# Splat attention with a following FFN on one Trainium2 core: output products due four key tiles sooner, denominators inverted after a block transposition, and another closing part

## The reference

```python
x = L0_attn_x                                   # (4, 2048, 256), float32
x = x + attn(layernorm(x))                      # 16 heads of 16
x = x + ffn(layernorm(x))

# attn: q, k, v from qkv_w; centers, scales, amplitudes of 16 splats for each head
q_weights = exp(q_dists * inv_var)              # squared distance of q to each center
k_weights = exp(k_dists * inv_var)
logits = einsum('bihs,bjhs,hs->bijh', q_weights, k_weights, amplitudes)
attention = softmax(logits / temp, axis=2)
out = einsum('bijh,bjhd->bihd', attention, v).reshape(Bx, Tx, Dx) @ out_w.T

# ffn: a shifted mix of each row with the row before it
xr = mu_r * x + (1 - mu_r) * x_prev;  xk = mu_k * x + (1 - mu_k) * x_prev
r = sigmoid(xr @ W_r.T);  k_act = square(relu(xk @ W_k.T))
out = r * (k_act @ W_v.T)
```

## Time and profile before

| | |
|---|---|
| median of three runs | 2170.7 us |
| profiled execution, and its span | 2168.94 us, 2167.2 us |
| TensorE matmul busy | 2132.7 us, 98% of the span |
| ScalarE busy | 2015.0 us, 93% |
| VectorE busy | 901.6 us, 42% |
| GpSimd busy | 393.0 us, 18% |
| the 2048 exponentials start | from 63.9 to 2125.5 us |
| granted TensorE clock, mean | 0.998 |

### The profile page before, as it was taken

One profiled execution on the slowest core, in us unless ns is written; L12 is line 12 of the kernel. 1 busy time (PEld: TensorE's weight loads), 2 busy tenths in 40 slices (PEclk: granted clock), 3 DMA queues, 4 the chain that ended last, 5 costly groups with the idle time before them and its releaser, 6 DMA issues.

```text
span 2167.2 us, 52662 instructions
## 1 busy us (share of the span) xinstructions
PE 2132.7 (98%) x22996; PEld 979.0 (45%) x22996; DVE 901.6 (42%) x1868; ACT 2015.0 (93%) x2194; POOL 393.0 (18%) x490
## 2 busy tenths in 40 slices
PE   8999999999999999999999999999999999999998
PEld 5444444444444444444444444444444444444445
DVE  6334544344443443444424344326333333424335
ACT  3899999999999999999999999999999999999994
POOL 0244243342100142022101203320310000000001
PEclk9999999999999999999999999999999999999999
DMA  6645435463321344316031432522261041311111
GB/s 179 164 123 151 113 110 123 131 154 104 92 46 47 92 118 101 97 41 179 24 89 29 128 77 87 123 87 79 59 158 52 22 87 50 53 29 50 33 40 49
DMA packets 176474, 193.34 MB, mean 89 GB/s; under 512 B 88640, under 2 KB 108480, under 8 KB 176224
## 3 DMA queue, kind: packets, MB, share of 16 engines
q1 hardware_dynamic: 166960, 174.96, 30.0%
q0 software_dynamic: 7168, 14.69, 2.9%
q10 hardware_dynamic: 2096, 0.14, 0.1%
HBM read 99.03 MB, written 75.94 MB: 81 GB/s over the span
## 4 chain that ended last, share of the span: by engine, by line
PE 90%; ACT 6%; DVE 2%; issue 1%; DMA 0%; SPq 0%; POOL 0%; DVEq 0%; POOLq 0%
PE ps_pv L886 40%; PE ps_scores L867 27%; PE ps_step L914 17%; ACT probs L1206 6%; PE ps_step L935 2%; PE ps_scores L899 1%; PE ps_scores L904 1%; PE ps_step L893 1%; ACT weight L1270 0%; PE ps_scores L909 0%; PE ps_scores L908 0%; DMA attn<-attn_kept 0%; DVE weight L1486 0%; DMA x_prep<-x 0%; DVE ffn_stats L1389 0%
## 5 line engine op out<-in xcount | busy, mean ns | idle before, releaser
L1206 ACT ACTIVATE probs<-ps_scores 128x1024 f32<-128x1024 f32 x2048 | 1940.9, 1031 | 84.0 <-PE ps_scores L867 58.6
L886 PE MATMUL ps_pv<-probs,vals 128*32 128x512 f32 (+5 forms) x10104 | 1079.9, 520 | 0.1
L867 PE MATMUL ps_scores<-q_aug,k_aug 49*128 49x512 f32 x4096 | 707.0, 442 | 8.0 <-ACT probs L1206 5.8
L867 PEld LDWEIGHTS ps_scores<-q_aug,k_aug 49*128 49x128 f32 x4096 | 331.8, 184 | 616.6 <-ACT probs L1206 562.7
L886 PEld LDWEIGHTS ps_pv<-probs,vals 128*32 128x32 f32 x10104 | 349.8, 139 | 200.3 <-issue 116.8
L1336 POOL DMA_DIRECT2D packed<-qk x224 | 113.0, 510 | 872.8 <-DVE qk L1509 851.0
L1341 POOL TENSOR_TENSOR packed<-qk 32x512 f32<-32x512 f32 x224 | 239.6, 1070 | 16.9
L1715 DVE RECIPROCAL den_all<-den_all 128x128 f32<-128x128 f32 x252 | 224.1, 924 | 0.6
L1346 POOL TENSOR_TENSOR k_act<-k_act 128x512 f32<-128x512 f32 x28 | 30.1, 1076 | 815.7 <-DVE k_act L1512 815.7
L1576 DVE COPY o_raw<-ps_pv 128x512 f32<-128x512 f32 x64 | 44.3, 692 | 246.9 <-PE ps_pv L886 246.3
L1486 DVE TENSOR_SCALAR weight<-ps_step,cen_sq 128x512 f32<-128x512 f32 x57 | 42.8, 751 | 185.2 <-PE ps_step L935 184.3
(11 more groups left out here) (218 smaller groups left out, 1116.1 us busy)
## 6 DMA issues: line engine op xcount, KB each, us to landing
k_aug<-k_parts SPq DMA_DIRECT2D x128, 192.0 KB, 4.7
q_aug<-q_parts SPq DMA_DIRECT2D x128, 192.0 KB
k_parts<-parts SPq DMA_DIRECT2D x32, 512.0 KB, 3.1
q_parts<-parts SPq DMA_DIRECT2D x32, 512.0 KB, 4.0
packed<-qk POOLq DMA_DIRECT2D x224, 64.0 KB, 2.3
x_ffn<-x SPq DMA_DIRECT2D x18, 512.0 KB, 4.8
k_parts<-parts SPq DMA_DIRECT2D x32, 256.0 KB, 3.8
q_parts<-parts SPq DMA_DIRECT2D x32, 256.0 KB, 4.4
```

What stands on the lines that cost most here:

```text
L867: mm = pe.matmul(ps_scores[:, g % RING, e, :], k_aug[rows, s % 2, pair, kt * P:(kt + 1) * P], q_aug[rows, u % 2, pair, :], start=True, sto ...
L886: mm = pe.matmul(ps_pv[32 * c:32 * c + 32, at], vals[:, s % 2, kt, :, c], probs[:, tick % PROB_SLOTS, c, at], start=(kt == 0), stop=(kt == ...
L1206: act.activation(probs[:, tick % PROB_SLOTS, 2 * pair:2 * pair + 2, :], ps_scores[:, g % RING, :, :], ACT.Exp).then_inc(probs_ready, 1)
```

## The change

Three things are changed together.

- `OUT_TICKS` goes from (17, 14) to (13, 10). The planner lays out all side work anew from this, so steps of many tasks stand at other ticks from tick 222 to 752 and from 938 to 1016. What stands between and before is as it was.
- The inverse: `spread` becomes a transposition of 32x32 blocks (one 128x512 instruction), after which each denominator stands once in every 32nd column. One reciprocal of 128x16 inverts them at the next tick, and a second transposition, of a broadcast view, spreads them over `den_all`. The multiply comes two ticks behind `spread` rather than six, and the store three ticks behind it rather than seven.
- The closing part: the last unit isn't copied out of `ps_pv` (no `take`); its transposition and its multiplies read PSUM. The last chunk's attn rows of stages 0 and 1 are loaded once, inside the loop (`LAST_ATTN_AT`), and the unit before the last is read from `o_raw`, not from DRAM. The second-to-last chunk's mixes are made by VectorE, not by ScalarE and GpSimd, its k products come ahead of its r products, and the last output rows are gated, finished and stored in three parts (two tiles, one, one) rather than two.

```diff
-OUT_TICKS = (17, 14)
-INVERT_PARTS = 4
+OUT_TICKS = (13, 10)
+LEFT_TICKS = 3
+INVERT_STEPS = 2
+LAST_ROWS = (slice(0, 2), slice(2, 3), slice(3, 4))
+LAST_ATTN_AT = end(LAST_BUT, "out1") + 1
...
@@ sync
-                for u in LEAVE_AT.get(tick - INVERT_PARTS - 3, ()):
-                    store_attn(u)
+                for u in LEAVE_AT.get(tick - LEFT_TICKS, ()):
+                    if UNIT[u] != (LAST[1], STAGES - 2, LAST[2]):
+                        store_attn(u)
+                if tick == LAST_ATTN_AT:
+                    for odd in range(2):
+                        done = UNIT_OF[LAST[1], odd, LAST[2]]
+                        sp.wait_ge(attn_stored[done % 2], ATTN * (done // 2 + 1))
+                    sp.wait_ge(step_mm, STEP_NO[LAST_BUT, "out1"] + 1)
+                    sp.dma_start(out=attn[:, 0, :], in_=attn_kept[LAST[1], 0:P, LAST[2] * CHUNK:(LAST[2] + 1) * CHUNK]
+                                 ).then_inc(attn_loaded, 16)
-            for odd in range(2):
-                sp.wait_ge(attn_stored[odd], ATTN * ((UNITS - 2 - odd) // 2 + 1))
-            sp.wait_ge(step_mm, STEP_NO[LAST_BUT, "out1"] + 1)
-            sp.dma_start(out=attn[:, 0, :], in_=attn_kept[b, 0:P, at]).then_inc(attn_loaded, 16)
-            for c in range(HEADS):
-                sp.dma_start(out=attn[32 * c:32 * c + S, 1, :], in_=attn_kept[b, P + 32 * c:P + 32 * c + S, at]).then_inc(attn_loaded, 16)
@@ tensor, closing part
-            pe.wait_ge(attn_loaded, 16 * n + 16 * (1 + HEADS))
+            pe.wait_ge(attn_loaded, 16 * (n + 1))
+            pe.wait_ge(scaled, UNITS - 1)
-                pe.matmul(banks[t][:, 0:D], attn[:, 1, t * P:(t + 1) * P], wout_last[:, 0, :], start=False, stop=False)
+                pe.matmul(banks[t][:, 0:D], o_raw[:, (UNITS - 2) % 2, at], wout_last[:, 0, :], start=False, stop=False)
-            pe.wait_ge(pv_free, UNITS)
-            pe.wait_ge(last_added, 2)
-            closing("r0", 7)
-            closing("r1", 6)
+            pe.wait_ge(last_mixed, 3)
+            closing("k0", 7)
+            closing("k1", 6)
             pe.wait_ge(last_evicted, 1)
-            pe.wait_ge(last_added, 4)
-            closing("k0", 0)
-            closing("k1", 1)
+            pe.wait_ge(last_mixed, 5)
+            closing("r0", 0)
+            closing("r1", 1)
@@ vector
-                v.stream_shuffle(den_all[:, :], o_raw[:, u % 2, :], odd_den if UNIT[u][1] % 2 else even_den).then_inc(den_spread, 1)
+                v.transpose(den_all[:, :], o_raw[:, u % 2, :]).then_inc(den_spread, 1)
+
+            def invert(u):
+                one = 0 if UNIT[u][1] % 2 else S
+                v.wait_ge(den_spread, u + 1)
+                v.reciprocal(den_columns[:, :], den_all[:, one:CHUNK:32]).then_inc(den_inverted, 1)
+
+            def replicate(u, at):
+                blocks = slice(at.start // 32, at.stop // 32)
+                columns = den_columns[:, blocks].unsqueeze(2).broadcast_to([P, blocks.stop - blocks.start, 32])
+                return v.transpose(den_all[:, at].rearrange("p (n t) -> p n t", t=32), columns)
...
-                for u in LEAVE_AT.get(tick - INVERT_PARTS - 2, ()):
-                    v.wait_ge(den_inverted, INVERT_PARTS * (u + 1))
+                for u in LEAVE_AT.get(tick - 1, ()):
+                    invert(u)
+                    v.wait_ge(den_inverted, INVERT_STEPS * u + 1)
+                    replicate(u, slice(0, CHUNK)).then_inc(den_inverted, 1)
+                for u in LEAVE_AT.get(tick - LEFT_TICKS + 1, ()):
+                    v.wait_ge(den_inverted, INVERT_STEPS * (u + 1))
                     v.tensor_tensor(o_raw[:, u % 2, :], o_raw[:, u % 2, :], den_all[:, :], ALU.mult).then_inc(scaled, 1)
-                for part in range(INVERT_PARTS):
-                    for u in LEAVE_AT.get(tick - 2 - part, ()):
-                        at = slice(part * CHUNK // INVERT_PARTS, (part + 1) * CHUNK // INVERT_PARTS)
-                        v.wait_ge(den_spread, u + 1)
-                        v.reciprocal(den_all[:, at], den_all[:, at]).then_inc(den_inverted, 1)
@@ vector, closing part
-            spread(u)
-            v.wait_ge(den_spread, u + 1)
+            v.wait_ge(pv_done, UNITS)
+            v.wait_ge(scaled, u)
+            v.transpose(den_all[:, :], ps_pv[:, :]).then_inc(den_spread, 1)
+            invert(u)
+            v.wait_ge(den_inverted, INVERT_STEPS * u + 1)
             for pair in range(2):
-                v.reciprocal(den_all[:, at], den_all[:, at]).then_inc(den_inverted, 1)
-                v.wait_ge(den_inverted, INVERT_PARTS * u + pair + 1)
-                v.tensor_tensor(last_o[:, at], last_o[:, at], den_all[:, at], ALU.mult).then_inc(scaled, 1)
+                replicate(u, slice(pair * CHUNK // 2, (pair + 1) * CHUNK // 2)).then_inc(den_inverted, 1)
...
+                v.tensor_tensor(last_o[:, at], ps_pv[:, at], den_all[:, at], ALU.mult).then_inc(scaled, 1)
+            for nth, part in enumerate((2, 3, 0, 1)):
+                v.wait_ge(last_copied, 3 + nth)
+                mixed(part, last_tmp[part]).then_inc(last_mixed, 1)
```

More of the change, by code:

```diff
@@ L1178, in _ @@
             closing("v1", 3)
[L1180 to L1181 removed]
+            pe.wait_ge(last_copied, 8)
+            pe.wait_ge(last_mixed, 8)
             closing("k0", 7)
             closing("k1", 6)
[L1184 to L1185 removed]
+            pe.wait_ge(last_copied, 12)
+            pe.wait_ge(last_mixed, 10)
             closing("r0", 4)
             closing("r1", 5)
+            pe.wait_ge(last_copied, 10)
             pe.wait_ge(last_evicted, 6)
[L1189 to L1190 removed]
+            for part, rows in enumerate(LAST_ROWS):
+                for t in range(rows.start, rows.stop):
+                    mm = rows_out(k_act, wv, t, 0, banks[part])
+                mm.then_inc(last_mm, 1)
         @block.scalar
@@ L1280, in last_old @@
                                    scale=one_minus_mu[:, which, half:half + 1]).then_inc(last_copied, 1)
-            def last_new(which, to):
-                for half in range(HALVES):
-                    act.activation(to[:, half, :], h2_t[:, half, 1:1 + CHUNK], ACT.Copy,
-                                   scale=mu[:, which, half:half + 1]).then_inc(last_copied, 1)
             def last_gate(pair, bank):
```

85 lines of the change are left out of this document (36 added, 49 removed).

## The result

The changed kernel takes 2179.2 us, the median of six runs (2178.3 to 2181.6). Six runs of the kernel before, timed beside it, gave 2170.6 us (2169.9 to 2170.9). The ratio is 1.0043, with a 95% interval of 1.0032 to 1.0053: the change makes the kernel slower by 8.6 us. The forecast was 2173.5 us, its range 2167.5 to 2178.5; the time lies above both, and slower by over 0.2% had a chance of 0.37.

The account below looks back on a forecast made before the run. It took TensorE and ScalarE, both nearly always busy, as the bound, VectorE mattering only by its order. Loop +9.0 and closing part -6.2 gave +2.8 us: 2173.5 us as a median, range 2167.5 to 2178.5.

Parts of the forecast that it names:

- plainly slower: every wait costs its clock as well: Rival: a lower clock follows each new wait in the loop; 2181 us, taken as 2178 with half the drops; chance 0.2.
- place A: Loop, tick 463: three mix parts behind the take delay the eviction of k0; TensorE waits 4.4 us; +5.3 us (3.8 to 6).
- Closing part: Behind the loop: no wait for attn from DRAM, so the last unit's products start 6.1 us sooner; -6.2 us (-4.5 to -7).
- The inverse: Loop, each unit: VectorE saves 2.7 us, hidden behind TensorE's work; 0 us, bounds -1 and +6.
- The rival of the dear transposition: Rival: a transposition takes 2.5 us, chains behind takes grow, the closing part keeps only 3 us; 2176 us, chance 0.08.
- Place B: Loop, ticks 271 and 319: a layer norm part delays v0's eviction; two waits of 1.4 us, +1.0 each, +2.0 (1 to 5).
- two more drops would come: Loop, ticks 271 and 319: if waits of 1.4 us also lower the clock, two more clock drops follow.
- Tick 612: Loop: a long VectorE chain delays v1's eviction of ffn (1, 1); wait 2.7, clock +1.3, less 0.9: +3.1 us (1.5 to 4.5).
- the 0.9 taken off: Loop, tick 612: 0.9 us subtracted because a step no longer ends in the boundary's gap.
- Two smaller ones: Loop: dist_q1 behind tick 387 and turn0 at tick 947 wait for eviction; 0 to 1.5 us each, together +1.0.
- Batch 3 side work moves forward: Loop, batch 3: side work four ticks sooner, into a thin stretch, evens out TensorE's load; -0.8 us (0 to -2).
- Gone, -1.6: Loop: the wait of 1.04 us at tick 249 and about 0.6 us in smaller ones disappear; -1.6 us.

Follow-up runs that it names:

- mixes alone moved: The changed kernel with only mixes 0, 1 and 2 of ffn (0, 3) moved from tick 463 to 464: 2174.4 us, ratio 1.0020.
- five parts moved: The changed kernel with three mixes of ffn (0, 3) and two layer norm parts (ticks 271, 319) one tick later: 2170.4 us, ratio 1.0002.
- The experiment: The changed kernel with OUT_TICKS (17, 10), so only batch 3's side work starts four ticks sooner: 2163.7 us, ratio 0.9973.
- all places moved: The kernel with five parts moved, plus mixes of ffn (0, 2) and (1, 2) and layer norm parts of ffn (3, 0) moved: 2163.4 us, ratio 0.9972.

## Why the prediction was wrong

The mechanism was right: VectorE's parts behind a take hold back evictions, and TensorE waits at the places named. The step that failed is the pricing of these waits, and beside it two gains that did not come. By the experiments' medians the waits cost 15.8 us (8.8 and 7.0), where the sum had 11.4 (5.3, 2.0, 3.1 and 1.0). And the sum took off 2.4 us (1.6 and 0.8) for what the new order gains, where the new order with its waits gone is 0.6 slower than the old one. The first is 4.4 us and the second 3.0, together the 7.4 us between the loop's +9.0 and the 16.4 measured.

The rival "plainly slower: every wait costs its clock as well" gave 2178 us, the nearest of the four, at a chance of 0.2. That nearness is in part luck: its mechanism did not hold as worded, since in the trace of the kernel after the clock fell behind two of the new waits, place A and tick 321, and not behind 273, 390, 612 and 947. Its full form (2181) was too much.

- **Closing part, -6.2: right.** 41.6 us from the last exponential's start to the end became 35.3, -6.4. By its steps: against the last exponential the output products start 4.4 us sooner and take 1.7 less at the full clock, so that the last unit's products are 6.1 us sooner, as priced, and their eviction too. One thing came unlooked for. Two of the layer norm's small instructions took 0.94 and 0.89 us rather than 0.17 while GpSimd's square ran, so the turn waited 1.14 us (2158.71) and came 5.4 us sooner, not 5.9. Putting the one load back behind the loop gives back 2.8 of the 6.4 us. The old kernel had five loads there and the lower clock behind them; no run puts the other four back, so how the remaining 3.6 us divide stays open.
- **The inverse, 0, bounds -1 and +6: right.** Transpositions of 0.70 us and a reciprocal of 0.25 for the 0.72 and 0.2 assumed; alone it gave -1.1 us, with an interval that holds 0. Its place in VectorE's list is another matter (0.8 us at tick 423 with the old order). The rival of the dear transposition falls by the first row. The Trainium skill, Vector Engine (DVE) Microarchitecture Reference, section "The reshape front-end and per-opcode configuration", gave one element per cycle per lane; the trace agrees, since a transposition of 512 columns takes 0.705 us where a copy of 512 takes 0.69.
- **Place A, +5.3: right.** A wait of 4.26 us for 4.4, and +5.7 us in the traces, +4.8 by the medians with the mixes alone moved.
- **Place B, +2.0 for two waits: mis-sized.** The waits were 1.15 and 1.18 us for 1.4. They cost 1.1 and 2.8 in the traces, and 4.0 by the medians of the kernels with five parts moved and with the mixes alone moved. The 1.0 each was right for a wait without its clock. But the clock fell behind the one at tick 321, for 1.7 us more; the text had said that "two more drops would come" if a drop followed so short a wait, and put 1 to 5 us on it, but the sum took none.
- **Tick 612, +3.1: mis-sized, and near in one trace by luck.** The wait was 3.23 us for 2.7. In the trace of the kernel after the clock stayed at 1.00 behind it and the price was 3.3. In two other traces the clock fell behind the same wait, and it cost 4.9 and 5.9. Of the 0.9 taken off for a step that no longer ends in the boundary's gap 0.4 shows: with the waits gone, the new order is that much better than the old over ticks 608 to 640, and 3.3 less 0.4 is the +2.9 of the first table.
- **"Two smaller ones ... together +1.0": mis-sized.** Tick 390 cost 1.3 us, with a wait of 1.15 to 1.17 us, and tick 947 cost 1.2, with one of 1.14 or 1.15: 2.4 together. I had put them at half of what the same reasoning gave at place B, on no row. Together with tick 612 the sum had 4.1; undoing the three gave 7.0 by the medians and 7.3 by the traces.
- **"Batch 3 side work moves forward ...: -0.8": no gain.** The experiment gives +0.9 for batch 3, the wait at 947 included. Even with the waits taken away, (13, 10) is no better than (17, 14): 2163.4 against 2162.8, and 2160.7 against 2159.2.
- **Gone, -1.6: not the order's.** The wait of 1.04 us went with the inverse alone as well, and with the old order and all else new; either way the exponentials were 1.1 us better off at tick 252. So it belongs to the inverse, which the sum had at 0. In the kernel after they are only 0.4 better off by tick 256, and nothing is seen of the 0.6 "in smaller ones".
- **Not in the sum at all:** +1.2 us between ticks 480 and 608, which no one wait makes up, and the start, +1.0. The first stands in the kernel with all places moved too, so it is the layout's, and its cause stays open. Of the second, half lies ahead of the first exponential and half behind it, where the clock is low for 6.8 us rather than 3.4. Low stretches of both lengths come there in the traces of kernels that are alike up to that point, so it is not the change's.

## What to carry to other kernels

An engine that works in order and stands at a wait has no slack there, however low its busy share: whatever is queued right behind the wait delays each result behind it one for one. So look for every eviction that stands behind such a wait, count the instructions between, and move those nobody wants soon to the other side of it; here a statistic, moved one tick, was worth more than a change of the whole layout. And where several places follow one pattern, price all of them from the same row, the small ones too: four waits of 1.14 to 1.18 us, priced at 0.5 to 1.0, cost 1.1 to 1.3 us each here, and one of them 2.8 where the clock fell behind it.
